# First layer: the target product stays in its PSUM bank until VectorE adds it, without ScalarE's copy

## What is computed

```python
def step(carry, inp):
    W, bb = carry
    xq_c, xk_c, xv_c = inp
    lr = jax.nn.sigmoid(jnp.einsum('bhkc,hcd->bhkd', xk_c, theta) + tb)
    eta = token_eta * (BASE_LR * lr / HD)
    Z1 = xk_c @ W + bb
    mu = Z1.mean(-1, keepdims=True)
    std = jnp.sqrt(Z1.var(-1, keepdims=True) + EPS)
    x_hat = (Z1 - mu) / std
    y = g * x_hat + be
    grad_output = y - (xv_c - xk_c)
    gxh = grad_output * g
    grad_x = (HD * gxh - gxh.sum(-1, keepdims=True) - x_hat * (gxh * x_hat).sum(-1, keepdims=True)) / (HD * std)
    dW = jnp.einsum('bhkc,bhkd->bhcd', eta * xk_c, grad_x)
    db = (eta * grad_x).sum(-2, keepdims=True)
    Wn, bn = (W - dW, bb - db)
    Zq = xq_c @ Wn + bn
    ...
    out = xq_c + g * ((Zq - mu2) / std2) + be
    return ((Wn, bn), out)
```

## Time and profile before

| | us |
|---|---|
| median of three runs | 970.23 |
| the profiled execution, its own time | 971.49 |
| its span in the trace | 969.3 |
| busy: TensorE / VectorE / ScalarE / GpSimd | 894.1 / 781.8 / 555.2 / 629.6 |
| mean granted TensorE clock | 0.979 of full speed |

### The profile page before, as it was taken

One profiled execution on the slowest core, in us unless ns is written; L12 is line 12 of the kernel. 1 busy time (PEld: TensorE's weight loads), 2 busy tenths in 40 slices (PEclk: granted clock), 3 DMA queues, 4 the chain that ended last, 5 costly groups with the idle time before them and its releaser, 6 DMA issues.

```text
span 969.3 us, 19700 instructions
## 1 busy us (share of the span) xinstructions
PE 894.1 (92%) x7768; PEld 617.4 (64%) x7768; DVE 781.8 (81%) x1182; ACT 555.2 (57%) x828; POOL 629.6 (65%) x571
## 2 busy tenths in 40 slices
PE   1687999999998897799999999999999999999997
PEld 1555778777786677556556656656656656666664
DVE  7768988998897635787887897888798788888876
ACT  3453666666664361456657656666655765756663
POOL 3357887888885002777668669568767866955872
PEclk9998999999999899799999999999999999999999
DMA  8100000000000301211011102101211111220110
GB/s 224 29 2 1 2 2 3 2 3 2 3 3 1 88 2 62 58 44 64 21 45 64 65 19 69 64 4 61 66 31 55 64 36 32 74 75 20 45 50 23
DMA packets 24962, 38.25 MB, mean 39 GB/s; under 512 B 9316, under 2 KB 15480, under 8 KB 22824
## 3 DMA queue, kind: packets, MB, share of 16 engines
q1 hardware_dynamic: 23240, 34.74, 11.7%
q10 hardware_dynamic: 1632, 2.27, 0.8%
HBM read 28.29 MB, written 1.43 MB: 31 GB/s over the span
## 4 chain that ended last, share of the span: by engine, by line
PE 60%; DVE 18%; issue 11%; POOL 6%; ACT 3%; DMA 1%; SPq 0%; POOLq 0%; DVEq 0%
PE bank L1142 12%; PE bank L1144 10%; PE bank L1143 10%; DVE hdh L958 5%; PE bank L1406 3%; PE bank L1298 3%; PE quad L1437 3%; PE quad L1194 3%; DVE add L967 2%; DVE mx L951 2%; PE quad L1185 2%; POOL arena L1068 2%; PE quad L1342 2%; PE bank L1257 2%; POOL arena L1062 2%
## 5 line engine op out<-in xcount | busy, mean ns | idle before, releaser
L951 DVE TENSOR_REDUCE mx<-quad 128x4 f32<-128x2048 f32 x64 | 146.4, 2288 | 41.4 <-PE quad L1437 41.3
L1113 POOL CAST hdh<-xn 128x512 fp32r<-128x512 f32 x96 | 65.7, 685 | 138.3 <-ACT xn L620 138.3
L635 ACT ACTIVATE ex<-quad 128x2048 f32<-128x2048 f32 x64 | 120.6, 1885 | 58.7 <-PE quad L1447 58.7
L1115 POOL TENSOR_TENSOR hdl<-hd,hdh 128x512 fp32r<-128x512 f32 x96 | 129.9, 1353 | 7.7
L1115 POOL TENSOR_TENSOR hdl<-xn,hdh 128x512 fp32r<-128x512 f32 x96 | 128.6, 1339 | 7.7
L1142 PE MATMUL bank<-hdh,W2h 128*128 128x512 f32 x256 | 113.1, 442 | 6.3 <-DVE hdl L961 4.1
L620 ACT ACTIVATE xn<-bank,b1c 128x512 f32<-128x512 f32 x128 | 88.0, 687 | 35.2 <-POOL hdl L1115 18.7
L620 ACT ACTIVATE hd<-bank,b1c 128x512 f32<-128x512 f32 x112 | 77.0, 688 | 45.1 <-PE bank L1144 26.8
L1144 PE MATMUL bank<-hdl,W2h 128*128 128x512 f32 x256 | 100.7, 393 | 0.0
L1143 PE MATMUL bank<-hdh,W2l 128*128 128x512 f32 x256 | 100.5, 393 | 0.0
L1142 PE MATMUL bank<-cH,W1h 128*128 128x512 f32 x192 | 81.0, 422 | 0.7 <-DVE cL L978 0.7
(11 more groups left out here) (304 smaller groups left out, 2205.5 us busy)
## 6 DMA issues: line engine op xcount, KB each, us to landing
cwB<-gate_rows SPq DMA_DIRECT2D x16, 1024.0 KB, 4.7
kx<-kqh SPq DMA_DIRECT2D x32, 64.0 KB, 2.1
qx<-kqh SPq DMA_DIRECT2D x32, 64.0 KB, 2.1
ex<-in_L_ffn_W SPq DMA_DIRECT2D x1, 1024.0 KB, 5.7
kx<-kql SPq DMA_DIRECT2D x16, 64.0 KB, 2.1
qx<-kql SPq DMA_DIRECT2D x16, 64.0 KB, 2.1
rec<-rec_rows SPq DMA_DIRECT2D x32, 32.0 KB, 2.1
out<-fin SPq DMA_DIRECT2D x4, 256.0 KB, 2.3
```

The lines of the kernel that those rows point to most:

```text
L635: act.activation(ex[:, t % 2, :, :], quad[:, :, :], ACT.Exp, scale=float(AD) ** -0.5).then_inc(ROUND["exps_ready"], 1)
L951: dve.tensor_reduce(mx[:, t, :, 0], quad[:, :, :], AX_X, ALU.max, negate=True).then_inc(ROUND["score_max"], 1)
L1113: pool.tensor_copy(hdh[:, m % RING, :], tile(n)).then_inc(ROUND["pool_split"], 1)
L1115: pool.tensor_tensor(hdl[:, m % RING, :], tile(n), hdh[:, m % RING, :], ALU.subtract).then_inc(ROUND["pool_split"], 1)
```

## The change

ScalarE's `take_u` and its semaphore `u_taken` are gone. VectorE's `gradient(s)` waits for `u_ready` and adds straight from `first_bank`. What waited for `u_taken` on TensorE (`target` and `keys`) now waits for `gx_ready`, which `gradient` signals.

```diff
@@ scalar engine @@
-            def take_u(s):
-                if s in LIVE:
-                    act.wait_ge(CHUNK["u_ready"], s + 1)
-                    act.activation(U[:, s % 4, :], first_bank[:, :], ACT.Copy).then_inc(CHUNK["u_taken"], 1)
-
...
-                take_xk(s), take_turned(s - 2), squares(s), squares_q(s), take_u(s)
+                take_xk(s), take_turned(s - 2), squares(s), squares_q(s)
@@ vector engine, gradient(s) @@
                     dve.wait_ge(CHUNK["scaled_ready"], s + 1)
-                    dve.wait_ge(CHUNK["u_taken"], s + 1)
-                    dve.tensor_tensor(gx[:, u, :], t1[:, u, :], U[:, u, :], ALU.add).then_inc(CHUNK["gx_ready"], 1)
+                    dve.wait_ge(CHUNK["u_ready"], s + 1)
+                    dve.tensor_tensor(gx[:, u, :], t1[:, u, :], first_bank[:, :], ALU.add).then_inc(CHUNK["gx_ready"], 1)
@@ tensor engine, target(s) @@
                     if s:
-                        pe.wait_ge(CHUNK["u_taken"], s)
+                        pe.wait_ge(CHUNK["gx_ready"], s)
@@ tensor engine, keys(s) @@
                 if 2 <= s <= 4 * NC - 3:
-                    pe.wait_ge(CHUNK["u_taken"], s + 1)
+                    pe.wait_ge(CHUNK["gx_ready"], s + 1)
                     features(first_bank, (s - 2) % 4, (s + 2) // 4, wkh, wkl).then_inc(CHUNK["keys_ready"], 1)
```

More of the change, by code:

```diff
@@ L277, in build @@
         rates_raw, rates_biased, rates_sigmoid, eta_ready = sem("rates_raw"), sem("rates_biased"), sem("rates_sigmoid"), sem("eta_ready")
-        N_CHUNKS = ("tokens_high", "tokens_low", "keys_ready", "keys_taken", "queries_ready", "queries_taken", "xk_ready", "xk_taken", "u_ready", "u_taken",
+        N_CHUNKS = ("tokens_high", "tokens_low", "keys_ready", "keys_taken", "queries_ready", "queries_taken", "xk_ready", "xk_taken", "u_ready",
             "z_ready", "z_squared", "z_sumsq", "z_dev", "z_rdev", "xhat_ready", "scaled_ready", "gx_ready", "gx_sum", "gx_centred", "rate_ready",
```

## The result

The changed kernel takes 1064.2 us (median of four runs, 1060.34 to 1064.81) beside 970.61 for the kernel before: a ratio of 1.0954, 95% interval 1.0925 to 1.0982. It is 94 us slower. 1047 was forecast, with 1028 to 1066 as the range. The profiled execution took 1064.81, its span 1062.7.

The account below looks back on a forecast made before the run. TensorE was taken as the bound of the recurrence, 30.84 of 31 us busy. Loop 66.4, less 1.1 for step 0, plus 12 for the clock made 77.3 us more, so 1047 us, range 1028 to 1066.

Parts of the forecast that it names:

- loop, steps 6 to 30: Recurrence: keys waiting for the gradient closes a loop through all four engines, 2.37 us more a step.
- loop, steps 2 to 5: First steps with keys, paced by VectorE's choice work: late keys partly absorbed, 2.4 us each, ends 0 and 7.
- clock: TensorE's new idle stretches in the recurrence lower its clock: 10 falls at 1.2 us, 12 us in all.
- head start: Step 0: the deviation's table load no longer stands behind the copy, 1.1 us gained, ends 0 and 1.9.
- K to z: Recurrence: from the first matmul of keys to the end of the next state products, 4.36 us.
- G to K: Recurrence: signal from the gradient's end to the first matmul of keys, 0.06 us.
- z to G: Recurrence: end of state products to end of gradient, 6.33, 4.99, 6.16 and 4.99 us over four steps.
- a time clearly under 4.99: Sign in even steps, state products' end to gradient's end: if under 4.99 us, the copy did matter.
- The add from PSUM: VectorE's gradient add with one operand in PSUM: no change from 0.69 us, 0.01 either way.
- faster: Rival: add ends before TensorE reaches keys, saving copy waits and table load, 1 to 6 us; chance 0.03.
- Half is absorbed: Rival: hidden TensorE slack or emptier engines absorb half of the recurrence's 66 us, giving 1002 us; chance 0.10.
- The clock stays low: Rival: TensorE's clock low in nearly all the recurrence, 1122 us, or 1074 with a fall each step; chance 0.09.

Follow-up runs that it names:

- clock held up: Changed kernel plus useless TensorE matmuls in the idle time ahead of each wait of keys: 1038.73 us, ratio 1.0698.
- the kernel with the copy kept: Kernel before with its copy of U and add from memory, but keys and target waiting for gx_ready: 1070.41 us, ratio 1.1009.
- the bank separate: Changed kernel with keys in half banks of their own, issued and taken earlier, dW waiting for that take: 974.01 us, ratio 1.0036.
- keys later and filler: Changed kernel with keys(s) issued after dW(s-2) and turn(s-1), plus useless matmuls ahead of dW: 1011.96 us, ratio 1.0433.
- the kernel with keys later: Changed kernel with keys(s) issued after dW(s-2) and turn(s-1) instead of ahead of them: 1044.93 us, ratio 1.0758.

## Why the prediction was right, and where it was off

The direction, the mechanism and the range held. The time was 17 us short, and the terms of the sum show where (differences of the two spans; the forecast's split is 24 and 4 steps of its 2.37):

| term | forecast | measured | by |
|---|---|---|---|
| loop, steps 6 to 30 | +56.9 | +54.2 | clock held up, 239.05 against 184.89 |
| loop, steps 2 to 5 | +9.5 | +9 to +11 | estimate, what the clock leaves of 22.9 |
| clock | +12 | +32 to +34 | 20 in steps 6 to 30, changed against filled; 12 to 14 in steps 2 to 5, estimate |
| head start | -1.1 | -2.4 | end of step 2's products |
| after step 30 | 0 | -1.3 | 681.0 against 682.3 |
| sum | +77.3 | +93.4 | |

**The loop** was right piece by piece. K to z was taken as 4.36 and is 4.37 at full clock. G to K was 0.06 and is 0.05 to 0.06 in all 28 steps. z to G was 6.33, 4.99, 6.16 and 4.99, and is 6.33, 4.88, 5.97 and 5.05 (steps 13 to 16; 4.89 in step 20, the next of its kind). So it did fall from 5.90 with VectorE relieved. (The delays of the list of steps 13 to 16 add up to 10.2, or 10.4 with the signals, and not to 10.3; nothing hangs on it.)

**The copy hid behind other work**, but for 0.1 us. z to G in an even step like 14 is 4.97 to 4.99 in each kernel with the copy and 4.87 to 4.91 in each without it, and the prediction had named a time clearly under 4.99 as the sign that the copy mattered. What failed is "VectorE is in L813 until 166.28 and can take the reciprocal only then": the rows there overlap by 0.09 (L751 starts at 165.00 and takes 0.69, L813 starts at 165.60), so VectorE was free some 0.09 before 166.28, and the deviation's end at 166.24 held it. In a loop that is 0.1 us in every second step, and more after a slow stretch, as the kernel with the copy kept shows. Where the loop is cut and TensorE sets the pace it is nothing: with the bank separate, steps 6 to 30 take 185.6 us without the copy and 184.9 with it.

**The add from PSUM**: L772 with one operand in the bank has a median of 686 ns and L777 with both in memory had 692 to 693. The 65 ns more that I worked out from the page "VectorE: DVE Perf Modes" of the Trainium skill (section on the TRN2 errata) are not there; the row decides. The line in the changed kernel (count, shortest/median/longest ns, first and last start):

```profile
L772 DVE TENSOR_TENSOR arena<-arena,bank x32: 678/686/689, 50.6 to 393.2; 128x512 f32<-128x512 f32 x32
```

**The clock was mis-sized**, in the price and hardly in the number. The step that failed is "so I take 1.2 a fall. [...] I take 10". There were 12 falls, 8 in the 24 steps from 6 on and one in each of steps 2 to 5, and they cost some 2.7 us each. I counted a fall as 3.3 us of low clock, after the earlier trace rows, and let part of it lie off the path. But all that follows keys up to z is work for TensorE on the loop, and it can grow to 7.7 us and still be at half clock: the row 127.60:135.00 is low throughout. From step 6 on K to z is above 4.4 in eight steps (7.7 us in three, 5.8 to 6.4 in five). What the clock slows ahead of the deviation is paid as well: z to G of step 5 is 7.72 instead of 6.33, of step 7 6.98.

In steps 2 to 5 K to z is 9.93, 6.82, 7.58 and 7.68 us. At full clock the same lists took 7.04 (step 2 of the kernel before, 65.11 to 72.15) and 3.96 (step 3 with filler), and I take the steady 4.37 for steps 4 and 5. That is 12.3 us of low clock, or 13.7 with z to G of step 5, and leaves 9 to 11 of the 22.9 to the late keys. It is an estimate, since no kernel kept full clock there. The nearest, with keys later and filler, had 0.94 and took 47.15 us for steps 2 to 5, 7.5 above the kernel before; with the 0.95 a step that the later keys won there it would be 11.3. So the mean of 2.4 that I took for these steps was about right. Keys would have been late by 7.0, 7.2, 6.3 and 3.5 us in them, 24 in all (from the timeline of before), and most of that was indeed absorbed: z to G of steps 3 and 4 fell from 11.37 and 8.65 to 7.32 and 5.40, as VectorE had its choice work done while the rest waited.

That the measured time lies in the range is in part luck. The upper end of 1066 was meant for 25 falls at 1.2 us; it was nearly reached by 12 falls at more than twice that.

The Trainium skill ("TensorE: Matmul & The Clock Gate", HAM oscillation) describes a loop whose clock falls in every turn, with waits of some 3 to 5 us. I had read it as a rule for any loop with a wait. Here, with waits of 0.5 to 3.1 us, the clock fell in 8 of 24 steady steps, so this case bears out the mechanism but not a fall in each turn.

Of the rivals, "faster" needed the gradient ahead of keys, which no step has. "Half is absorbed" is refuted by the filled kernel, whose four steps take what the sum says. "The clock stays low" holds for steps 2 to 6 (0.64) but not for the rest (0.90).

## What to carry to other kernels

A copy out of PSUM buys the time at which the bank is free again. Before dropping one, look for who writes the bank next and how late the other reader is: compare the start of that write with the end of the read in the timeline, step by step. If the read is later, the engine that writes joins a loop with all that the reader waits for, and the loop's length is the sum of its pieces and not the busiest engine's time. With a spare half bank for the other tenant, the same removal cost nothing (969.3 us against 971.4, a lead that an edit of step 0 alone gives in part). When a dense TensorE gets waits of 2 to 3 us, price the slow clock as well: everything between the wait and the next product at up to 1.8 times its length (7.68 for 4.37), which here added more than a third of what the loop itself did in steady steps, and by the estimate above at least as much as the loop in the first four.

## What the runs showed of the hardware

- Useless matmuls ahead of a wait made the kernel faster: 1064.2 to 1038.7 with keys in place, 1044.9 to 1012.0 with keys later. In each the granted clock of the steady steps was 1.00.
- An idle stretch of 1.8 to 1.9 us before dense work was enough for the clock to fall within some 2 us behind it, in two of four steady steps of the kernel with keys later. In the kernel before, 1.2 us was not the earlier trace rows.
- In the changed kernel, steps 6 to 29, the clock fell behind 8 of the 12 waits of 2.5 to 3.1 us and behind none of the 12 of 0.5 to 1.4 us; with the copy kept, 9 of 12 and none.
- A shorter wait was not cheaper in proportion: the kernel with keys later waited 34 us in all for the gradient (and 10 for the take of the keys, which is new), the changed one 65, and yet it gained only 19 us. Some 4 us in four of its steps were low clock.
- What decides behind which of the longer waits the clock falls stays open. It differs between executions of one kernel: with the copy kept they ran from 1062.7 to 1074.3 us, at mean clocks of 0.943 and 0.927.
